# Two layers of attention: VectorE does the null column and the value row first in its step, and POOL's mask addition waits for the subtraction of the maximum

## What is computed

```
q = (xn @ Wq), 16 heads of 64;  k, v = xn @ Wkv, one head shared by all 16
k, v get one "null" key and value ahead of the 64 tokens
layer 0: q, k normalised to length 1, sim = 8 q k^T;  layer 1: sim = q k^T / 8
sim = sim + bias (null column: a constant of each head);  masked and causal: -inf
attn = softmax(sim) over 65 columns;  out = attn @ v @ Wout;  layer norm
```

## Time and profile before

| | us |
|---|---|
| median of 3 runs | 1653.41 |
| lowest, highest | 1652.0, 1655.38 |
| profiled execution, first to last instruction (span) | 1601.1 |
| median less that span | 52.3 |

### The profile page before, as it was taken

How to read it: one execution, slowest core, us unless ns; L and a number is a source line. 1 busy time by engine, 2 the same in 40 slices (tenths; PEclk the granted TensorE clock), 3 DMA queues, 4 the chain that set the end, 5 groups by cost and what they waited for, 6 DMA issues and landing times.

```text
span 1601.1 us, 43442 instructions
## 1 busy us (share of the span) xinstructions
PE 1360.7 (85%) x15406; PEld 1185.1 (74%) x15407; DVE 1259.5 (79%) x2281; ACT 882.6 (55%) x2216; POOL 885.6 (55%) x871
## 2 busy tenths in 40 slices
PE   1898999999759999968999999858998279999994
PEld 0787887788648888857888888747887168888883
DVE  4499999999954989899999999847886697454457
ACT  1456566656536666734556656536876156444544
POOL 1477767776614555535555555547885114777723
PEclk9899999999988999988999999988999589999997
DMA  7210000000103000000000000110002321333355
GB/s 194 33 33 8 9 7 8 8 8 8 33 5 74 1 0 0 1 2 8 9 9 8 9 9 9 26 41 15 14 14 67 111 80 51 96 95 95 95 164 167
DMA packets 89654, 65.03 MB, mean 41 GB/s; under 512 B 50833, under 2 KB 84372, under 8 KB 89493
## 3 DMA queue, kind: packets, MB, share of 16 engines
q1 hardware_dynamic: 82578, 44.98, 10.3%
q0 software_dynamic: 6912, 17.84, 3.6%
HBM read 39.18 MB, written 18.35 MB: 36 GB/s over the span
## 4 chain that ended last, share of the span: by engine, by line
PE 47%; DVE 28%; ACT 12%; issue 8%; POOL 2%; DMA 1%; SPq 1%; DVEq 0%; ACTq 0%; POOLq 0%
PE psW L1871 8%; PE psQ L2142 8%; PE psQ L1792 6%; PE psW L2124 4%; DVE ex L1252 3%; PE psS L1853 2%; DVE count L1437 2%; ACT oT L911 2%; PE psS L1886 2%; DVE ex L1246 2%; DVE ex L1250 2%; DVE step L1443 2%; DVE den L1297 2%; PE psT L1829 2%; ACT sqT L867 2%
## 5 line engine op out<-in xcount | busy, mean ns | idle before, releaser
L679 POOL TENSOR_TENSOR pn<-ex,rden 128x1024 f32<-128x1024 f32 x64 | 136.8, 2138 | 226.0 <-PE psT L1829 221.9
L1871 PE MATMUL psW<-wout,oT 128*128 128x256 f32 x1536 | 210.9, 295 | 43.3 <-ACT oT L911 41.2
L1792 PEld LDWEIGHTS psQ<-xT,wq 128*128 128x128 f32 x1536 | 206.1, 205 | 53.5 <-issue 51.1
L1871 PEld LDWEIGHTS psW<-wout,oT 128*128 128x128 f32 x1536 | 196.2, 197 | 61.8 <-ACT oT L911 55.3
L1792 PE MATMUL psQ<-xT,wq 128*128 128x256 f32 x1536 | 226.0, 301 | 9.0 <-DVE xT L1334 9.0
L2142 PE MATMUL psQ<-W,exT 128*128 (+1 forms) x624 | 172.6, 412 | 0.1
L687 POOL TENSOR_TENSOR masked_bias<-bias_t,negmask 128x1024 f32<-128x1024 f32 x64 | 146.0, 2281 | 17.7 <-DVEq L1258 9.0
L723 POOL TENSOR_TENSOR hT<-hf,hT 128x512 fp32r<-128x512 f32 x64 | 98.3, 1537 | 102.3 <-ACT hT L988 102.3
L2142 PEld LDWEIGHTS psQ<-W,exT 128*128 128x128 f32 x624 | 110.9, 191 | 19.4 <-issue 0.4
L1263 DVE TENSOR_TENSOR ex<-ex,m 128x1040 f32<-128x1040 f32 x64 | 111.9, 1749 | 2.2
L796 POOL DMA_INDIRECT rows<-xf,src x72 | 72.4, 1006 | 72.5 <-issue 58.8
(11 more groups left out here) (304 smaller groups left out, 3598.1 us busy)
## 6 DMA issues: line engine op xcount, KB each, us to landing
both<-results SPq DMA_DIRECT2D x16, 512.0 KB, 8.3
raw_w<-W SPq DMA_DIRECT2D x27, 256.0 KB, 4.6
vv<-vp SPq DMA_DIRECT2D x256, 16.0 KB, 1.8
xf<-xf_all SPq DMA_DIRECT2D x4, 1024.0 KB
out<-X SPq DMA_DIRECT2D x8, 512.0 KB, 2.9
X<-x SPq DMA_DIRECT2D x1, 3584.0 KB, 15.9
raw_q<-Wq SPq DMA_DIRECT2D x2, 1024.0 KB, 6.4
bvv<-v_all SPq DMA_DIRECT2D x128, 16.0 KB, 1.8
```

Source lines behind the costliest of these rows:

```text
L679: nc.gpsimd.tensor_tensor(pn[:], ex[t % 2][:, :, 0:S], rden[:].unsqueeze(2).to_broadcast([P, H, S]), ALU.mult).then_inc(sem("t_pn"), 1)
L1792: mm = nc.tensor.matmul(psQ[:, cc, h * QT:h * QT + QT], wq[w][:, k, c * P:c * P + P], xT[g % 2][u][:, k, :], start=(k == 0 and j == 0), st ...
L1871: mm = nc.tensor.matmul(psW[:, 0:D], oT[u][:, c, :], wout[w][:, c, :], start=(u == 0 and c == 0 and w == 0), stop=(u == 1 and c == CH - 1))
```

## The change

Four orders change in VectorE's list, and one wait on POOL:

- `vp` of tile i-1 is now made at the head of step i; before, `vp` of tile i was made after the subtraction in step i.
- The null column (L1247 and L1252, in layer 1 L1256) now stands ahead of the scores (L1246, in layer 1 L1255) and ahead of the wait for them.
- Nothing else stands between L1250 and the maximum L1261 any more.
- POOL's `masked_bias` waits for `t_sub`, the end of L1263, where it waited for `t_sum`, the end of L1250 (in layer 1 of L1255).

No instruction is added or removed.

```
@@ POOL, attention, step @@
-                        reach(pool, sem("t_sum"), done + t)
+                        reach(pool, sem("t_sub"), done + t)
                         nc.gpsimd.tensor_tensor(masked[:], bias_t[:], negmask[:, t:t + 1, :].to_broadcast([P, H, S]),
                                                 ALU.add).then_inc(sem("t_bm"), 1)
@@ VectorE, attention, step @@
                     norm_stats(done, i + 4)
                     norm_moments(done, i + 4)
+                    t = i - 1
+                    if live(t):
+                        dve.wait_ge(sem("t_kvs"), done + t + 1)
+                        if t >= VP:
+                            dve.wait_ge(sem(f"t_vv{(t - VP) % VV}"), v_there(done, t - VP))
+                        nc.vector.tensor_tensor(vp[t % VP][:], kvs[:, DH:2 * DH], nvb[:], ALU.subtract).then_inc(sem("t_vp"), 1)
                     t = i - 2
                     if live(t):
+                        e = ex[t % 2]
+                        reach(dve, sem("t_pn"), done + t - 1)
+                        if L["cosine"]:
+                            dve.wait_ge(sem("t_rq"), t + 1)
+                            nc.vector.tensor_tensor(e[:, :, S], sn[t % 2][:], rq[t % 2][:], ALU.mult).then_inc(sem("t_snr"), 1)
+                            dve.wait_ge(sem("t_snr"), t + 1)
+                            nc.vector.tensor_tensor(e[:, :, S], e[:, :, S], nbias[:], ALU.add).then_inc(sem("t_null"), 1)
+                        else:
+                            nc.vector.tensor_tensor(e[:, :, S], sn[t % 2][:], nbias[:], ALU.add).then_inc(sem("t_null"), 1)
                         dve.wait_ge(sem("t_sp"), done + t + 1)
-                        reach(dve, sem("t_pn"), done + t - 1)
-                        e = ex[t % 2]
                         if L["cosine"]:
-                            dve.wait_ge(sem("t_rq"), t + 1)
...
-                            nc.vector.tensor_tensor(e[:, :, S], sn[t % 2][:], rq[t % 2][:], ALU.mult).then_inc(sem("t_snr"), 1)
...
-                            dve.wait_ge(sem("t_snr"), t + 1)
-                            nc.vector.tensor_tensor(e[:, :, S], e[:, :, S], nbias[:], ALU.add).then_inc(sem("t_null"), 1)
                         else:
...
-                            nc.vector.tensor_tensor(e[:, :, S], sn[t % 2][:], nbias[:], ALU.add).then_inc(sem("t_null"), 1)
...
-                        dve.wait_ge(sem("t_kvs"), done + t + 1)
-                        if t >= VP:
-                            dve.wait_ge(sem(f"t_vv{(t - VP) % VV}"), v_there(done, t - VP))
-                        nc.vector.tensor_tensor(vp[t % VP][:], kvs[:, DH:2 * DH], nvb[:], ALU.subtract).then_inc(sem("t_vp"), 1)
```

## The result

The changed kernel takes 1693.66 us (1692.06 to 1696.54, 4 runs) against 1652.7 (1646.6 to 1655.38, 4 runs): the ratio is 1.0245, with a 95% interval of 1.0225 to 1.0264. That is 41 us slower; the forecast was 10, and its range ended at 1689.

A forecast was written before the change was run, and what follows sets the result against it. PE was taken to bound layer 1, the chain through the engines layer 0. Layer 0's 375.5 against 364.3 us, less 2 for the last tile, gave + 9, layer 1 0: 1653.4 + 9 = 1663 us, range 1652 to 1689.

The forecast's parts named there:

- S: Layer 0: the end of the subtraction L1263, from which the prediction counted a step's times up to the next such end.
- upper bound of 2.1: Layer 0, odd tiles: the qmx clamp, just behind masked_bias's start, is held until masked_bias ends, 2.1 us.
- even step: Layer 0 step without clamps: L1290 isn't held, PE is late, pn runs during L1246, subtraction ends at 12.67.
- ramp: Layer 0's first three tiles: pn follows rq at once and holds L1247; 13.5 us each.
- 21 x 12.44 = 261.2: Layer 0's steady intervals: 21 at 12.44 us per tile, from a pair of odd and even steps of 24.89.
- PE's round without waits 11.03: Layer 0: PE's time per tile free of waits, 12.34 - 1.31 = 11.03 us, used to place pn in even tiles.
- 4 x 12.05 at the end: Layer 0's end: four intervals of 12.05 us, where no norm root is left in POOL's chain.
- left at 13.3: Layer 0: the interval up to 433.4, with feed-forward weights, taken as unchanged at 13.3 us.
- PE busy 200.00 of 200: Layer 1: PE is full and sets the pace, so some 2 us of VectorE saved per tile give 0.
- Rival 1: Layer 0: pn gets in front of VectorE's additions every step, about 13.5 us per tile; + 33, 1686 us; chance 0.33.
- Rival 2: Layer 0: POOL gives way, pn never costs VectorE anything, 11.92 us per tile; 1646 us; chance 0.10.
- Rival 3: Layer 0: no change, pn comes after L1250 in all steps, 12.22 us per tile; 1654 us; chance 0.12.

The follow-up runs named there:

- filler: Changed kernel, with PE doing the first 16 output-projection matmuls twice in odd steps of layer 0; 1676.53 us, 1.0121 of the kernel before.
- wait_only: Kernel before, with only POOL's wait changed (t_sub in place of t_sum) and VectorE's order kept; 1622.68 us, 1.015 of the kernel before.
- order_only: Changed kernel, with POOL's mask addition waiting for t_sum as before, so only VectorE's order differs; 1595.59 us, 0.9972 of the kernel before.
- Stall: Kernel before, plus one useless VectorE instruction of 3.35 us ahead of L1290 in odd steps of layer 0; 1722.14 us, 1.0399 of the kernel before.
- clamps_late: Changed kernel, with the clamps (qmx) moved behind the two instructions of L1294; 1634.24 us, 1.0226 of the kernel before.
- rq_first_before: Kernel before, with POOL doing rk, norm root and rq ahead of the mask addition in layer 0; 1671.83 us, 1.0113 of the kernel before.

## Why the prediction was wrong

**What held.** `masked_bias` at S + 0.08. L1248 at S + 6.54, forecast and filler run alike. The clamp, for which the trace of before had no row and I took the upper bound of 2.1: the first of L1286's two takes 2.08 to 2.10 in all but the first step. The Trainium skill (VectorE: DVE Perf Modes, Mode 2×_2P) lets a one-source SBUF instruction with an even outermost count use both ports; the rows agree, for the 64x32 clamp in wait_only (2.14) as well. `pn` at S + 8.33 (forecast 8.31), next S at 12.26 (12.22), and the even step 12.54 (12.67). L1250 is not held in any but one tile (0.19). The ramp's first three intervals: 13.53, 11.90, 14.15, in sum 39.6 for 40.5; that the sum is near is in part luck, as each was to be 13.5. Where the clock stays up the 21 steady intervals sum to 262.7 us in the filler run, one disturbed stretch of three tiles among them (+ 2.8); the forecast had 261.2. Wait_only shows that the moved wait is the main cost, + 31 us on its own, and order_only that the order is not. Had the two parts added up, layer 0 would have lost 26 us and not 37: the standstill of 2.6 us comes with both together alone (1.1 and 1.5 us before the same wait with one).

**What held in number only.** By the forecast `rq` was what L1248 waits for, 1 to 2 us in every tile. In the filler run VectorE waits for it 0.85 us in the even steps and not at all in most odd ones, in which the held clamp had made VectorE's own list as late; in the changed kernel it waits in 3 steps of the window 120:370, 2.6 us in all. So the moved wait costs through the clamp as much as through `rq`. The terms of layer 0 add to 375.1, not 375.0, which changes nothing.

**The step that failed** is the term "21 x 12.44 = 261.2" of the sum for layer 0, by what it left out. The same 21 intervals take 283.5 us in the profile after: + 22.3. I had L1290 ending at S + 3.79 in odd steps and asked only when `pn` could start. PE had been done with its first 16 matmuls since about S + 1.2 (248.05 in the step above, S = 246.80), so it must stand for 2.6 us, and "PE's round without waits 11.03" was taken from rows at a granted clock of 1.00. After such a standstill the clock falls in 6 of 9 cases and PE works at half speed for 3.4 to 10.2 us. Where it is 6.8 us the pair takes 28.3 us for 24.8, 3.5 more; where it is 10.2, 28.9. Two runs show the cause from both sides. Filler cuts the standstill from 2.6 to 0.7 us and takes away nothing else of the change: 23.8 us of layer 0 come back. Stall puts a standstill into the kernel before: the same fall, 2.1 to 3.2 us a time. "Wrong if" in the prediction doesn't name it either.

**Smaller terms.** 4 x 12.05 at the end became 51.5 us (+ 3.3, one more slow stretch; filler 48.3). The interval that was left at 13.3 is 14.7 (+ 1.4). The last tile doesn't give back 2: its interval is 15.12 against 14.65. With the ramp's - 0.9 and the 22.3 above, these terms make + 28.7 and take the forecast for layer 0 from + 9 to the 37.4 measured.

**Layer 1** moved by 0.2 us, as forecast, but not for the reason given. "PE busy 200.00 of 200" did not mean that nothing could be gained: the interval fell from 10.20 to 10.03. The groups of the window 800:1000, in the kernel before and in the one after:

```profile
L1871 PE MATMUL psW<-wout,oT 128*128 128x256 f32 x480 | 63.9, 289 | 0.0
```

```profile
L1875 PE MATMUL psW<-wout,oT 128*128 128x256 f32 x480 | 61.7, 284 | 0.0
```

The 24 matmuls of a tile take 3.19 us before and 3.08 after, and a wait of a tenth inside or ahead of such a group is counted as busy. In the timeline of before ScalarE's L911, which they need, ends 0.05 us ahead of them and L1290 1.9 after their start; in the one after 0.21 ahead and 0.7 after. So VectorE's and ScalarE's lateness reached PE by some 0.17 us per tile. Order_only has one without the other, L911 0.21 ahead and L1294 1.9 after: its group takes 3.12 us and its tile 10.06, so 0.14 of the 0.17 go with ScalarE. That is a reading; no run was made to try it. VectorE itself has room: in order_only its subtraction is held there for 2 us in most tiles (3.22 for 1.24), and the tile is still shorter than before's. In the ramp the gain is lost again: three intervals of 9.73, 9.73 and 10.83 for 8.12, 8.12 and 8.68. With `masked_bias` moved, the norm root ends late, and `pn` starts right behind it, 0.06 ahead of `xn`. Timeline of the changed kernel:

```profile
771.18 1.90 POOL L679 TENSOR_TENSOR pn<-ex,rden 128x1024 f32<-128x1024 f32 x1
771.24 1.99 DVE L1317 TENSOR_SCALAR xn<-X,mv,rstd 128x256 f32<-128x256 f32 x1 [0.37 <-POOL rstd L641]
```

Wait_only pays nearly the same in two steps (9.57 each) and keeps 4.3 us in all. Order_only, where `masked_bias` isn't moved, takes 9.34, 9.34 and 10.12 there, so this is not the only way to lose it.

**The rivals.** Rival 1 had its condition right (clamps not held: 13.5 per tile) and nearly its price: clamps_late gives 13.53 in half of its tiles and loses 30 us in layer 0, for 33. It isn't what the changed kernel does. That rival 1's total, 1686, lies nearer to 1693.66 than the forecast is chance. Rival 2 fell: L1248, when 0.06 to 0.14 behind a POOL read, is held every time. Rival 3 fell as its counter-argument said: in the filler run's even steps `pn` starts at S + 7.00 (309.68, forecast 7.12), ahead of L1261.

**What stays open.** Of the 41 us, 37.4 lie in layer 0 and 0.2 in layer 1; the rest isn't located. Between the layers the kernel before itself takes 282.6 us in one profile and 279.2 in the other (the changed kernel 280.4), and behind the attentions there is no profile of it on a chip that takes 612 to 618 us there. Which of the standstills brings the clock down and which not is not settled: of equal ones of 2.6 us 6 in 9 do, and a second execution of the same kernel has other ones among the 6. In 120:370 none of order_only's 1.5 us standstills does, nor of rq_first_before's of 1.7, but 2 of clamps_late's of 1.9 do, for 3.4 us each.

## What to carry to other kernels

When a step makes another engine late, ask not only who waits, but for how long PE stands: behind 6 of 9 waits of 2.6 us PE worked at half speed for 3.4 to 10.2 us, and each fall of 6.8 us or more cost the changed kernel's chain 3.5 us or more. Between VectorE and POOL none of the orders tried here removed the conflict, they only chose who pays: `pn` and `masked_bias` read for 4 us of each 12, and an instruction with two SBUF tiles, the clamp L1286 or `xn`, when it started 0.06 to 0.14 us behind one of them, was held to its end. The sums and maxima (TENSOR_REDUCE) and the scores' multiplication from PSUM kept their 1.2 us there. Check each part of such a change alone: here one part gave 0.3%, the other gave 4.3 us in one layer and took 31 in the other, and the parts that gain, together, beat both kernels by 0.4% and 2.9%.

## What the runs showed that I had not expected

- PE's granted clock falls in the middle of a dense stage: a standstill of 2.59 us (248.04 to 250.63), then 0.50 until 261.6. A standstill of the same length at 277.4 had no such effect.
- More matmuls can make a kernel faster: 16 extra in each odd step, 20.6 us less.
- The same kernel takes 1597 us on one chip and 1654 to 1655 on two others. The attentions agree to 0.4 us on the chips on which it was profiled, and kernels profiled on the others take some 55 us longer behind the attentions.
